# Second expert layer with both fp16 parts of the weights in one 256-column product

## What is computed

```python
x = x + gnn(layernorm(x), adj)      # masked tanh(adj * adj), top 350 of a row, relu
xn = layernorm(x)
topk_scores, topk_idx = top_k(xn @ Wg.T + bg, 2)
combine = sum(softmax(topk_scores)[..., None] * one_hot(topk_idx, 8), axis=-2)
for e in range(8):
    h = relu(xn @ W1[e].T + b1[e])            # 512 wide
    y = h @ W2[e].T + b2[e]                   # 128 wide
    out = out + combine[..., e:e + 1] * y
x = x + out
```

## Time and profile before

| | |
|---|---|
| median of 3 runs | 514.0 us |
| lowest and highest run | 513.38 and 514.96 us |
| span of the profiled execution, first to last instruction | 457.2 us |
| around the span, against the median | 56.8 us |
| mean granted TensorE clock | 0.962 of 2.4 GHz |
| busy: TensorE, VectorE, ScalarE, GpSimd | 395.6, 355.8, 334.3, 208.3 us |

### The profile page before, as it was taken

How to read it: one execution, slowest core, us unless ns; L and a number is a source line. 1 busy time by engine, 2 the same in 40 slices (tenths; PEclk the granted TensorE clock), 3 DMA queues, 4 the chain that set the end, 5 groups by cost and what they waited for, 6 DMA issues and landing times.

```text
span 457.2 us, 8102 instructions
## 1 busy us (share of the span) xinstructions
PE 395.6 (87%) x2493; PEld 239.8 (52%) x2493; DVE 355.8 (78%) x866; ACT 334.3 (73%) x333; POOL 208.3 (46%) x276
## 2 busy tenths in 40 slices
PE   0899999999698969999999979979897989999800
PEld 0455544444243334465445534436796989998600
DVE  5999978986999999995799999999978444443235
ACT  1889998979977957959999996985554656665300
POOL 3049961000001810560381365882777777777500
PEclk9999999999889979999999999999999999999955
DMA  7829987775567746875688486953764464432069
GB/s 224 341 102 378 355 296 238 288 282 185 183 196 257 246 176 193 300 264 211 224 289 330 145 302 219 369 163 56 104 115 156 96 121 104 98 87 52 13 234 323
DMA packets 54627, 95.03 MB, mean 208 GB/s; under 512 B 34292, under 2 KB 41640, under 8 KB 46384
## 3 DMA queue, kind: packets, MB, share of 16 engines
q1 hardware_dynamic: 43584, 79.40, 53.1%
q0 software_dynamic: 5856, 12.71, 9.1%
q10 hardware_dynamic: 5136, 2.30, 1.7%
HBM read 77.90 MB, written 12.27 MB: 197 GB/s over the span
## 4 chain that ended last, share of the span: by engine, by line
DVE 47%; PE 29%; issue 11%; DMA 5%; ACT 3%; POOL 2%; ACTq 1%; SPq 1%; DVEq 0%; POOLq 0%
DVE marks L894 17%; PE bank L1407 6%; PE bank L1497 4%; PE bank L1523 3%; PE bank L1499 3%; PE bank L1498 3%; PE bank L1522 3%; PE bank L1524 3%; ACT tbuf L1147 3%; DMA tbuf<-expert_rows 2%; DVE rowbf L748 2%; DVE nrm L822 2%; PE bank L1352 2%; DVE w2h L902 1%; DVE stats L713 1%
## 5 line engine op out<-in xcount | busy, mean ns | idle before, releaser
L1407 PE MATMUL bank<-tbuf,g_sb 128*128 128x512 f32 x512 | 237.8, 611 | 1.4 <-ACT g_sb L1167 0.7
L1407 PEld LDWEIGHTS bank<-tbuf,g_sb 128*128 128x128 f32 x512 | 95.0, 195 | 106.0 <-issue 100.0
L659 POOL DMA_INDIRECT routed_rows<-aug,slots x64 | 88.2, 1378 | 104.6 <-DVE base L872 87.0
L894 DVE SCALAR_TENSOR_TENSOR marks<-abuf,marks 128x2048 bf16<-128x2048 int32 x56 | 129.4, 2311 | 1.0
L1147 ACT ACTIVATE tbuf<-abuf 128x2048 f32<-128x2048 f32 x64 | 121.5, 1898 | 5.0 <-PE bank L1407 2.6
L1151 ACT ACTIVATE tbuf<-tbuf 128x2048 f32<-128x2048 f32 x64 | 122.3, 1910 | 2.0
L673 POOL DMA_INDIRECT expert_rows<-abuf,xmeta x72 | 70.8, 984 | 25.1 <-issue 17.3
L1065 DVE SCALAR_TENSOR_TENSOR tbuf<-bank,tbuf 128x512 f16<-128x512 f32 x72 | 46.7, 685 | 43.6 <-ACT tbuf L1254 43.3
L1522 PE MATMUL bank<-w2h,tbuf 128*128 x288 | 51.7, 219 | 3.2 <-DVE tbuf L1065 3.2
L1524 PE MATMUL bank<-w2h,tbuf 128*128 x288 | 51.5, 219 | 0.0
L1523 PE MATMUL bank<-w2l,tbuf 128*128 x288 | 51.5, 219 | 0.0
(11 more groups left out here) (231 smaller groups left out, 445.2 us busy)
## 6 DMA issues: line engine op xcount, KB each, us to landing
abuf<-in_adj_tiles SPq DMA_DIRECT2D x64, 1024.0 KB, 5.3
wstage<-in_w POOLq DMA_DIRECT2D x16, 256.0 KB, 6.0
tbuf<-expert_rows SPq DMA_DIRECT2D x8, 512.0 KB, 6.2
out<-xres ACTq DMA_DIRECT2D x8, 256.0 KB, 6.3
routed_rows<-pad SPq DMA_DIRECT2D x9, 130.0 KB
expert_rows<-abuf,xmeta POOLq DMA_INDIRECT x72, 2.4
routed_rows<-aug,slots POOLq DMA_INDIRECT x64
abuf<-routed_rows SPq DMA_TRANSPOSE x40
```

The source lines that it names most:

```text
L659: pool.indirect_dma_start(xs, bass.IndirectOffsetOnAxis(ap=slots[:, q, k * SUB + cc:k * SUB + cc + 1], axis=0), aug[:, q, k, cc, :], None) ...
L894: dve.scalar_tensor_tensor(mark, bits_in, 1.0, mark, ALU.min, ALU.add).then_inc(s_raw, 1)
L1407: last = pe.matmul(ps_feat[ib % 2][:, :], g_sb[:, c, :], tbuf[:, buf, cc, :], start=(c == 0), stop=(c == C - 1))
```

## The change

Both parts of the second layer's weights lie side by side in one tensor, so that hs is multiplied by both in one product of 256 columns; hs x low lands in columns of its own, and is no longer summed up with the other two inside the bank. ScalarE scales and stores the first part as before, and VectorE then reads the second from the bank, scales it and adds it (`add_low`, two instructions of 128x128 per tile), after `cut_h` of the tile that follows. GpSimd waits for VectorE's addition where it waited for ScalarE. Tiles take turns at banks 4 and 6 (5 and 7 for second halves), and `layer2(t)` waits for tile t - 2 only. Two small results of the stream move from bank 6 to bank 5, for which `block_counts` of the last block waits for `add_features` of that block.

```diff
@@ -95,7 +95,7 @@
         g_sb = sb("g_sb", [P, C, D])
         feat_t = sb("feat_t", [P, N])
         w1h, w1l = sb("w1h", [P, E, H], fp16), sb("w1l", [P, E, H], fp16)
-        w2h, w2l = sb("w2h", [P, E, HB, D], fp16), sb("w2l", [P, E, HB, D], fp16)
+        w2hl = sb("w2hl", [P, E, HB, 2, D], fp16)
         wstage = sb("wstage", [P, 4, PW])
         abuf = sb("abuf", [P, NBUF, CK, IW])
         tbuf = sb("tbuf", [P, NBUF, CK, IW])
@@ -245,18 +245,22 @@
 
         ps_ncand = bank[7][:, 0:4]
         ps_tie = bank[7][:, 8:10]
-        ps_flag = bank[6][:, 200:202]
+        ps_flag = bank[5][:, 200:202]
         ps_rowt = bank[7][:, 128:256]
         ps_fixrow = bank[7][0:R, 256:256 + D]
         ps_fixt = bank[7][:, 384:384 + P]
-        ps_y, ps_y2 = bank[4][:, 0:2 * D], bank[5][:, 0:D]
-
-        def y_half(t, s):
-
-            return ps_y2 if s and t % NT >= NF else ps_y[:, s * D:(s + 1) * D]
+
+        def y_bank(t, s):
+
+            own = t % NT >= NF
+            at = bank[4 + 2 * (t % 2) + (s if own else 0)]
+            return at[:, 0:2 * D] if own else at[:, s * 2 * D:(s + 1) * 2 * D]
+
+        def y_part(t, s, v):
+            return y_bank(t, s)[:, v * D:(v + 1) * D]
 
         def counts_of(ib):
-            return bank[6][:, 192:192 + SUB] if ib == NB - 1 else ps_cnt[ib % 2][:, 0:SUB]
+            return bank[5][:, 192:192 + SUB] if ib == NB - 1 else ps_cnt[ib % 2][:, 0:SUB]
 
         def ps_h(q, half):
             return bank[q + 2 * half]
@@ -359,6 +363,7 @@
         s_relu = sem("s_relu")
         s_hs = sem("s_hs")
         s_y = sem("s_y")
+        s_ya = sem("s_ya")
         s_yo = sem("s_yo")
         s_sc = [sem(f"s_sc{i}") for i in range(NX)]
         s_yl = [sem(f"s_yl{i}") for i in range(NK)]
@@ -896,8 +901,8 @@
             def split_piece(i):
                 j = i % NPC
                 if i < NPC:
-                    hi, lo = w2h[:, j, :, :].rearrange("p b d -> p (b d)"), w2l[:, j, :, :].rearrange("p b d -> p (b d)")
-                    src = wstage[:, i % 4, :]
+                    hi, lo = w2hl[:, j, :, 0, :], w2hl[:, j, :, 1, :]
+                    src = wstage[:, i % 4, :].rearrange("p (b d) -> p b d", d=D)
                     dve.wait_ge(s_wst[i % 4], (i // 4 + 1) * 16)
                     dve.tensor_scalar(hi, src, WS, None, ALU.mult).then_inc(s_whi, 1)
                     dve.wait_ge(s_whi, i + 1)
@@ -1066,8 +1071,17 @@
                                              0.0, hh[:, q, hb, :].rearrange("p h s -> p (h s)"),
                                              ALU.max, ALU.subtract).then_inc(s_hs, 1)
 
+            def add_low(t, u):
+                for s in range(2):
+
+                    dve.wait_ge(s_ya, t * 2 + (s + 1 if t % NT >= NF else 2))
+                    dve.scalar_tensor_tensor(ysb[:, u, s, :], y_part(t, s, 1), xmeta[:, t % NT, s, 1:2],
+                                             ysb[:, u, s, :], ALU.mult, ALU.add).then_inc(s_yo, 1)
+
             for t in range(NT):
                 cut_h(t, t % 2)
+                if t:
+                    add_low(t - 1, (t - 1) % NX)
                 ready_steps(FFN + t)
                 route_steps(FFN + t)
                 if t == COUNT:
@@ -1079,6 +1093,7 @@
                     last_tiles()
                 if FFN + t == END + 1:
                     last_halves()
+            add_low(NT - 1, (NT - 1) % NX)
 
             redo = read_redo(dve)
             with dve.If(redo > 0):
@@ -1122,6 +1137,9 @@
                 last_halves()
                 for t in range(NT, 2 * NT):
                     cut_h(t, t % 2)
+                    if t > NT:
+                        add_low(t - 1, (t - 1) % NX)
+                add_low(2 * NT - 1, (2 * NT - 1) % NX)
                 chain[:] = before_if
 
 
@@ -1259,8 +1277,8 @@
                     act.wait_ge(s_sc[u], t // NX * 32)
                 for s in range(2):
                     act.wait_ge(s_y, t * 2 + s + 1)
-                    act.activation(ysb[:, u, s, :], y_half(t, s), ACT.Copy,
-                                   scale=xmeta[:, t % NT, s, 1:2]).then_inc(s_yo, 1)
+                    act.activation(ysb[:, u, s, :], y_part(t, s, 0), ACT.Copy,
+                                   scale=xmeta[:, t % NT, s, 1:2]).then_inc(s_ya, 1)
 
             for t in range(NT):
                 relu_h(t, t % 2, fresh=t < 2)
@@ -1414,7 +1432,7 @@
                 if ib == 0:
                     pe.wait_ge(s_const, 1)
                 if ib == NB - 1:
-                    pe.wait_ge(routed.sl, NB - 1)
+                    pe.wait_ge(routed.x2, NB)
                 pe.wait_ge(s_raw, (ib + 1) * NK)
                 for s in range(SUB):
                     for cc in range(CK):
@@ -1502,26 +1520,27 @@
 
             def layer2(t, q, es, fresh=False):
                 if not fresh:
-                    pe.wait_ge(s_yo, t * 2)
+                    pe.wait_ge(s_yo, (t - 1) * 2)
+                elif t:
+                    pe.wait_ge(routed.sl, NB - 1)
                 n = 2 // len(es)
                 for g, e in enumerate(es):
 
                     at = range(g * n, (g + 1) * n)
-                    y = ps_y if n == 2 else y_half(t, g)
-                    pe.matmul(y.rearrange("p (s d) -> p s d", s=n), ones_h[:, :],
+                    y = bank[4 + 2 * (t % 2) + g]
+                    pe.matmul(y[:, 0:n * 2 * D].rearrange("p (s v d) -> p s v d", s=n, v=2)[:, :, 0, :], ones_h[:, :],
                               b2_hl[:, bass.ds(e, 1), :].to_broadcast([P, n, D]), start=True, stop=False,
                               skip_group_check=True)
                     for hb in range(HB):
                         if g == 0 and hb % 2 == 0:
                             pe.wait_ge(s_hs, t * 2 + hb // 2 + 1)
-                        hi = w2h[:, bass.ds(e, 1), hb, :].rearrange("p o d -> p (o d)")
-                        lo = w2l[:, bass.ds(e, 1), hb, :].rearrange("p o d -> p (o d)")
+                        hi = w2hl[:, bass.ds(e, 1), hb, 0, :].rearrange("p o d -> p (o d)")
+                        hi_lo = w2hl[:, bass.ds(e, 1), hb, :, :].rearrange("p o v d -> p (o v d)")
                         for s in at:
-                            dst = y_half(t, s)
                             hs, ls = hh[:, q, hb, s * P:(s + 1) * P], hl[:, q, hb, s * P:(s + 1) * P]
-                            pe.matmul(dst, hs, hi, start=False, stop=False, skip_group_check=True)
-                            pe.matmul(dst, hs, lo, start=False, stop=False, skip_group_check=True)
-                            last = pe.matmul(dst, ls, hi, start=False, stop=(hb == HB - 1), skip_group_check=True)
+                            pe.matmul(y_bank(t, s), hs, hi_lo, start=False, stop=False, skip_group_check=True)
+                            last = pe.matmul(y_part(t, s, 0), ls, hi, start=False, stop=(hb == HB - 1),
+                                             skip_group_check=True)
                     last.then_inc(s_y, n)
 
             def expert_tiles(run, beside):

```

## The result

The changed kernel takes **510.91 us** in the median of 8 runs (507.91 to 512.18), the kernel before 513.95 in 8 runs beside it (512.95 to 515.0): ratio 0.9929, 95% interval 0.9908 to 0.995, so faster by about 3.6 us by the ratio; the two medians lie 3.0 apart. I had said 517.2, range 514.2 to 520.2, and slower with 0.76.

What follows compares the result with a forecast made beforehand. TensorE was taken to bound the steady tiles, VectorE tiles 1 to 9. The terms 4.20 - 0.44 - 0.60 - 0.25 + 0.29 = +3.2 us, on the median of 514.0, gave 517.2 us, range 514.2 to 520.2.

Steps and rivals of the forecast that it cites:

- the 56.8 us around it stay: Outside the profiled span of 457.2 us: this time was taken as unchanged when going from span to the median of 514.0.
- My last line: Signs of being wrong: among them TensorE waiting in steady tiles, making VectorE's cover false and the time larger than the range.
- my own case: Whole kernel: the summed terms hold, 517.2 us, 514.9 to 519.7 with measurement allowance; chance 0.80.
- Additions, +4.20: VectorE, tiles 1 to 8: added work and waits delay routing and TensorE by 4.20 us, free from tile 10 on.
- my formula 1.68 + 6p: Delay through tile 8, p being VectorE's time per pair of additions: 3.5 us at p = 0.30, 5.0 at p = 0.56.
- The rival that idle time absorbs the additions: VectorE's gaps beside the early tiles take up the additions: 513.7 us, not slower, decided at tile 5; chance 0.15.
- Whole tiles, -0.44: TensorE, tiles 10 to 31: one wide product replaces two narrow, 0.02 us of 2.76 per tile, -0.44 us; bounds 0 and 1.
- The rival that loads bound TensorE: All 288 steps fall from 0.23 to about 0.17 us, since loads count: 501 us; chance 0.02.
- Half tiles, -0.60: TensorE, 20 steps until tile 34's first half: 0.20 us instead of 0.23 each, -0.60 us; bounds 0 and -1.2.
- My premise that two addresses are still computed: Half-tile steps on TensorE: the two kinds of product still name two addresses, so only 0.03 us per step goes.
- Banks, -0.25: Tile 35: its 0.54 us bank wait goes, but GpSimd's stores limit the gain to -0.25 us; nothing in steady tiles.
- The end, +0.29: Behind the last tile: the last additions stand between ScalarE and GpSimd, +0.29 us.

## Why the prediction was wrong, point by point

**The step that failed** is the reading of the profile, ahead of every term: "the 56.8 us around it stay". Span and median didn't belong together. On the first kind of chip the period is 4.05, not 2.88, and "in steady tiles no wait for the bank is left to remove, TensorE being always busy" is false there: TensorE is busy 14.95 of 20 us and waits 1.03 us for the bank in each tile, so that the banks that I had at -0.25 bring 10 us alone. The additions that I had at 4.5 with their end cost 10 there, and the merging, 1.0 in my sum, is worth 2 to 6. No term of my sum was made on the machine that was timed, and no rival had this mechanism. My last line had the sign for it, TensorE waiting in steady tiles, but read it as a larger time. A gap of 56.8 us between span and median should have cost my own case most of its chance.

What the sum was made for is the second kind, so its terms are held against that:

**Additions, +4.20 (and 0.29 at the end).** Right in size in one profile of the changed kernel, short by a third in the other. VectorE beside the tiles, in the former (40.3 in the table):

```profile
324.20 0.61 DVE L1078 SCALAR_TENSOR_TENSOR abuf<-bank,xmeta,abuf 128x128 f32<-128x128 f32 x2 [0.77 <-ACT abuf L1280]
324.73 0.68 DVE L812 TENSOR_TENSOR xres<-xres,bank 128x512 f32<-128x512 f32 x1
...
339.30 0.18 DVE L846 TENSOR_TENSOR scores<-bank,gate_b 128x32 f32<-128x32 f32 x1
...
342.90 0.18 DVE L801 TENSOR_REDUCE m<-masked 128x4 f32<-128x32 f32 x1
...
349.57 0.17 DVE L976 CAST pad_i<-base 1x8 int32<-1x8 f32 x1
...
355.40 0.14 DVE L992 TENSOR_TENSOR placed<-tiles,ends 1x8 f32<-1x8 f32 x1
```

Tile 0 starts 2.16 us later than in the profile of before (321.91 against 319.75). Less these, the first choice (tile 4) is 2.85 us later (predicted 2.0), the second (tile 5) 3.7 (2.83), `last_tiles` 4.4 (3.77) and `last_halves` 4.9 (4.19). `add_features` starts 2.65 us after `cut_h(1)`, 1.27 before: 1.38 later (1.31). One addition takes 345 ns (0.29) and a pair occupies 0.53 (p = 0.42), near the upper bound that I had taken from four instructions in 1.11. With p = 0.53 my formula 1.68 + 6p gives 4.9, and tile 10 starts 4.7 later. (Of the 1.68, 0.14 was a slip: I let `relu_h(6)` take 1.20 us, where the earlier trace rows have 1.06.) TensorE's wait in tiles 8 and 9:

```profile
354.50 0.39 PE L1541 MATMUL bank<-w2hl,tbuf 128*128 x1 [2.78 <-DVE tbuf L1070]
359.56 0.28 PE L1541 MATMUL bank<-w2hl,tbuf 128*128 x1 [0.77 <-DVE tbuf L1070]
```

Against the earlier trace rows these products are 4.4 and 4.8 us later (predicted 3.8 and 4.2). The rival that idle time absorbs the additions is refuted; the choice in tile 5, at +3.7, decides it as I had said. That they cost nothing from tile 10 on is shown by the kernel merged from tile 9.

My sum had no term for TensorE's clock. Behind the wait of 2.78 us the products run at the lower of its two levels, 1.2 GHz, a step of 256 + 128 columns in 0.32 us instead of 0.17:

```profile
354.79 0.42 PE L1541 MATMUL bank<-w2hl,tbuf 128*128 x1
355.00 0.31 PE L1542 MATMUL bank<-w2hl,tbuf 128*128 x1
```

Here it cost nothing, since TensorE had to wait for VectorE again in tile 9. In the other profile `layer2(9)` begins as late after tile 0 (37.6 us in both), but the clock is down behind it (mean 0.94 from 360 to 380 us, 1.00 in this one), `layer1(11)` takes 2.6 instead of 1.3 us, and tile 10 starts 41.8 us after tile 0 instead of 40.3. So idle time that the additions make can cost again by the clock, 1.5 us here.

**Whole tiles, -0.44.** The period is as predicted, 2.74:

```profile
387.57 0.27 PE L1531 MATMUL bank<-b_hl,ones_h 128*128 x1
387.68 0.27 PE L1541 MATMUL bank<-w2hl,tbuf 128*128 x1
387.79 0.22 PE L1542 MATMUL bank<-w2hl,tbuf 128*128 x1
387.85 0.27 PE L1541 MATMUL bank<-w2hl,tbuf 128*128 x1
...
390.31 0.27 PE L1531 MATMUL bank<-b_hl,ones_h 128*128 x1
```

A step of 256 + 128 columns takes 0.17 us, as three of 55.8 ns did. The rival that loads bound TensorE is refuted. The Trainium skill's page "TensorE: Matmul & The Clock Gate", section "Back-to-back issue gap", has about 81 ns for 128 columns with a load each; the starts here are 0.05 to 0.06 apart, so the trace disagrees with it. But 1.6 us were won from tile 10 to 31 (against the banks alone; 2.0 with them), not 0.44. I had missed the places where TensorE's queue has more to do than the products: from tile 15 to 16, where the queue loads the coming tiles' experts, the period was 4.21 and is 3.46, with a stop of 1.28 us before and 0.55 after, and from tile 30 to 31, with the first half tile's layer 1 in it, it was 3.71 and is 3.01. Before:

```profile
372.03 0.28 PE L1497 MATMUL bank<-abuf,w1h 128*128 128x256 f16 x1 [1.28 <-issue]
```

After:

```profile
378.04 0.28 PE L1515 MATMUL bank<-abuf,w1h 128*128 128x256 f16 x1 [0.55 <-DVE tbuf L1070]
```

**Half tiles, -0.60.** This term was mis-sized most: from tile 31 to the last half, the changed kernel needs 11.9 us and the one with only the banks 15.1, so merging is worth 3.2. Weight loads of one half:

```profile
424.37 0.10 PEld L1542 LDWEIGHTS bank<-w2hl,tbuf 128*128 128x128 f16 x1
424.48 0.10 PEld L1541 LDWEIGHTS bank<-w2hl,tbuf 128*128 128x128 f16 x1
424.53 0.10 PEld L1542 LDWEIGHTS bank<-w2hl,tbuf 128*128 128x128 f16 x1
424.64 0.10 PEld L1541 LDWEIGHTS bank<-w2hl,tbuf 128*128 128x128 f16 x1
```

A step takes 0.16 to 0.17, down to its columns, where the earlier trace rows have 0.23 and I took 0.20. My premise that two addresses are still computed was wrong, and the profiles of before and of the result show it in TensorE's queue (`PEldq`). Before, L1522 and L1523 had 160 such instructions each; after, L1541 has 160 and L1542 none:

```profile
L1523 PEldq ALU_OP  x160: 32/32/32, 319.2 to 432.5; - x160
```

```profile
L1541 PEldq FUSED_REGOPS  x160: 46/46/46, 320.8 to 478.8; - x160
```

The kernel with the wide product split again has 160 on each of two lines once more, and its steps in half tiles take 0.25. And I counted 20 steps to the first half of tile 34, though the last half sets the end.

**Banks, -0.25.** -1.0 by the times (interval down to nothing), -1.1 by the traces, 0.7 of it in the half tiles: small, as said, on this kind.

**The end, +0.29.** GpSimd's last stores:

```profile
432.99 0.98 POOL L678 DMA_INDIRECT expert_rows<-abuf,xmeta  x1 [0.91 <-DVE abuf L1078]
434.28 0.98 POOL L678 DMA_INDIRECT expert_rows<-abuf,xmeta  x1 [0.30 <-issue]
435.56 0.98 POOL L678 DMA_INDIRECT expert_rows<-abuf,xmeta  x1 [0.30 <-issue]
436.85 0.98 POOL L678 DMA_INDIRECT expert_rows<-abuf,xmeta  x1 [0.30 <-issue]
```

The last store follows the last half's bias product (432.6) by 4.2 us; before, it was 2.7 (431.7 to 434.36). The four stores of the last two tiles now run 1.29 apart without a gap: the half tiles come faster than GpSimd can store, and give back 1.5 us. I had named GpSimd as next in line and not followed it.

The terms of the traces on the second kind are then +4.7 - 1.6 - 3.2 - 1.1 (banks, 0.4 of it in whole tiles) + 1.5 = +0.3, against +3.2 predicted; in the profile with the late fall of the clock 1.5 more. The two timings, of other executions, gave +1.9 and -0.8.

**On the first kind** it is the merging that turns the sign: with the banks and the additions but three products the ratio is 1.0048, with the wide product 0.9929. The banks are not needed for it, since the changed kernel with the one bank's wait is at 0.9922, though alone they bring 0.978 to 0.981. Why the merging is worth 6 us there beside the additions and 2 to 3 without them, and the additions 10, is not shown.

## What to carry to other kernels

Before any sum is made from a profile, hold its span against the times of the runs: where they differ by more than a few us, the profile is of another regime, and a wait that it doesn't show may be in every tile. An operation put in front of a chain of dependent steps costs its full time there, and nothing a few tiles later; so apply such a change only where its engine has room. When products are merged, count the address instructions in TensorE's queue too, not only columns and loads. Follow each gain to the next engine in the queue, in the last tiles above all.

## What the runs showed that I had not expected

The same kernel takes 511 us on two chips and 461 to 462 on two others, by 50 us all beside the tiles. On the first kind ScalarE follows TensorE's last product of a tile by a median of 1.8 us, and once by 10, instead of 0.3, and single instructions of TensorE start 0.7 or 1.4 us apart with nothing to wait for. In such stretches the granted clock falls: 0.73 from 320 to 340 us, with TensorE busy 11.85 of 20 us. What makes the completions late is not settled: no experiment here touched it. The instructions themselves don't seem to come late: in the kernel before, queue q8, of kind instruction, has 24 packets and 0.39 MB on both kinds, with 0.3% of the DMA engines' time on the first and 0.4% on the second. Fewer instructions on TensorE go with a shorter time (merging, 2 to 6 us), but the recording of the profile may have a part in it too, and it wasn't tried without.
